# A new order of one attention unit on all five engines: the output projection a unit later and in another bank, the logits in the values' bank, no negation, GpSimd's row work in other places

## The reference, cut to what matters

```python
sa, ca, ga, sb, cb, gb = ...                   # from silu(c) @ wmod, per sequence; ga, gb kept away from 0
h = layernorm(x) * (1 + ca) + sa
Q, K, V = h @ Wq.T + bq, h @ Wk.T + bk, h @ Wv.T + bv     # 16 heads of 16; rotary positions on Q, K
weights = softmax(where(causal, Q @ K.T / 4, -1e9))
x = x + ga * ((weights @ V) @ Wo.T + bo)
h = layernorm(x) * (1 + cb) + sb
route = softmax(h @ switch_w + switch_b)       # 8 logits a token; the largest picks the expert
x = x + gb * (gelu(h @ w1[e] + b1[e]) @ w2[e] + b2[e]) * max(route)
```

## Time and profile before

| | |
|---|---|
| median of 3 runs | 783.38 us (782.95 to 783.81) |
| profiled execution, its own time | 782.81 us, span 781.0 us |
| mean granted clock of TensorE | 0.956 |
| busy, share of the span: TensorE | 677.4 us, 87% |
| VectorE | 601.2 us, 77% |
| ScalarE | 513.3 us, 66% |
| GpSimd | 475.3 us, 61% |

### The profile page before, as it was taken

How to read it: one execution, slowest core, us unless ns; L and a number is a source line. 1 busy time by engine, 2 the same in 40 slices (tenths; PEclk the granted TensorE clock), 3 DMA queues, 4 the chain that set the end, 5 groups by cost and what they waited for, 6 DMA issues and landing times. The chain is left out here.

```text
span 781.0 us, 21181 instructions
## 1 busy us (share of the span) xinstructions
PE 677.4 (87%) x7438; PEld 425.6 (55%) x7438; DVE 601.2 (77%) x1241; ACT 513.3 (66%) x1035; POOL 475.3 (61%) x609
## 2 busy tenths in 40 slices
PE   5766888899999999999999888855999999999993
PEld 4332444445454544545445444434787878788772
DVE  6577888989988989989889667248577777777774
ACT  2334888888888988889888878643444444444441
POOL 4422566788888888888978777841244453535331
PEclk9797999999999999999999999956999999999998
DMA  8103423334445543634536345339666642322100
GB/s 265 37 8 50 124 88 103 102 102 150 123 138 134 147 136 105 174 98 136 136 83 164 107 138 153 110 134 376 208 217 204 211 151 70 88 85 86 35 21 0
DMA packets 61363, 97.49 MB, mean 125 GB/s; under 512 B 8404, under 2 KB 42317, under 8 KB 60752
## 3 DMA queue, kind: packets, MB, share of 16 engines
q1 hardware_dynamic: 56272, 79.36, 34.5%
q0 software_dynamic: 4992, 16.79, 6.8%
HBM read 69.47 MB, written 34.51 MB: 133 GB/s over the span
## 5 line engine op out<-in xcount | busy, mean ns | idle before, releaser
L1150 DVE TENSOR_REDUCE row_max<-ps_max 128x2 f32<-128x768 f32 (+2 forms) x192 | 199.9, 1041 | 40.4 <-PE ps_max L672 40.3
L955 ACT ACTIVATE prob<-ps_sc 128x1024 f32<-128x1024 f32 (+1 forms) x192 | 169.7, 884 | 52.8 <-PE ps_sc L699 49.6
L1503 PE MATMUL ps_h<-tok_t,w_all 128*128 128x128 f16 x1872 | 156.3, 219 | 0.7 <-DVE tok_t L1678 0.5
L1503 PEld LDWEIGHTS ps_h<-tok_t,w_all 128*128 x1872 | 130.9, 98 | 41.9 <-issue 2.2
L1573 ACT ACTIVATE hid<-ps_h,b_t 128x128 f32<-128x128 f32 x312 | 89.3, 368 | 95.8 <-PE ps_h L1503 95.7
L441 POOL TENSOR_SCALAR_AFFINE_SELECT prob<-prob 128x512 f32<-128x512 f32 x128 | 87.0, 680 | 68.7 <-ACT prob L955 65.9
L1420 POOL DMA_INDIRECT slot_mem<-row_dram,token x39 | 55.8, 1430 | 119.3 <-DVE y L1713 99.4
L1516 PE MATMUL ps_y<-w_all,hid_parts 128*128 x312 | 118.0, 379 | 1.3 <-DVE hid_parts L1688 1.2
L665 PE MATMUL ps_max<-k_t,q_t 64*128 64x512 f16 (+3 forms) x512 | 69.0, 306 | 35.1 <-DVE row_max L1150 34.8
L712 PE MATMUL ps_pv<-prob,v_sb 128*32 128x512 f32 (+3 forms) x1024 | 90.3, 448 | 0.3
L1518 PE MATMUL ps_y<-w_all,hid_parts 128*128 x312 | 85.1, 273 | 0.0
(11 more groups left out here) (267 smaller groups left out, 1355.8 us busy)
## 6 DMA issues: line engine op xcount, KB each, us to landing
raw<-w SPq DMA_DIRECT2D x64, 256.0 KB, 3.0
w_dram<-halves SPq DMA_DIRECT2D x64, 256.0 KB, 3.3
w_all<-w_dram SPq DMA_DIRECT2D x20, 512.0 KB, 4.5
row_dram<-rows SPq DMA_DIRECT2D x32, 256.0 KB, 3.3
w_all<-w_dram SPq DMA_DIRECT2D x3, 2048.0 KB, 13.1
mod_rows<-mods_dram SPq DMA_DIRECT2D x16, 256.0 KB, 7.1
row_dram<-mods_dram SPq DMA_DIRECT2D x32, 128.0 KB, 4.8
xs<-x SPq DMA_DIRECT2D x24, 128.0 KB, 3.3
```

The lines of the kernel that those rows point to most:

```text
L955: nc.scalar.activation(p_kb[:, :, first * L:(first + n) * L], ps_sc[:, :, 0:n * L], ACT.Exp, scale=SCALE).then_inc(exp_done, 1)
L1150: nc.vector.tensor_reduce(dst, ps_max[:, :, 0:n * L].rearrange("p j (m l) -> p j m l", m=n), AX.X, ALU.max).then_inc(max_done, 1)
L1503: last = mm(o, w[:, :, k, f, :][:, bass.ds(e, 1), :].rearrange("p e m -> p (e m)"), tok_t[:, j % 2, piece, k, :], start=(n == 0 and f % HF ...
```

## The change

It reorders pieces of a unit and changes what they wait for:

- `project_out` and `residual` of a tile come a unit later, at s = 2 and s = 3, in columns of the query/key bank `ps_b` and not of `ps_nd`. The projection waits until the rotary work has read `ps_b`, and `q_transposes` until the residual has.
- The logits go to s = 4 and 5 of the unit before, in the values' bank `ps_a`.
- `maxima` writes into `q_aug` itself; the `negated` step is gone and the keys' constant column holds -1 instead of 1.
- The bias product of the query/key projection goes ahead to s = 0. On VectorE `statistics` goes to s = 0, `divide` to s = 2 and `residual` to s = 3. On ScalarE the second scaling of the second weight piece goes behind `keep_shift`.
- GpSimd: the unit begins with the former unit's last `low_piece`, then `low_h`, `row_power`, `row_hat`; `row_modulate` stands behind `rotate`; `gate_weights` and `add_const` stand behind `low_piece(2 * U)`, ahead of `clear_future(2)`.

The diff, cut to its core:

```diff
@@ GpSimd, setup
-            nc.gpsimd.memset(k_aug[:, :].rearrange("p (h w) -> p h w", w=HW)[:, :, 3 * DK:3 * DK + 1], 1.0).then_inc(consts_done, 1)
+            nc.gpsimd.memset(k_aug[:, :].rearrange("p (h w) -> p h w", w=HW)[:, :, 3 * DK:3 * DK + 1], -1.0).then_inc(consts_done, 1)
@@ GpSimd, units
             for U in range(NU):
-                T = U + LEAD
-                if U >= QT - 1:
-                    add_const(U - QT + 1)
+                T, Y = U + LEAD, U - QT - 2
+                if U:
+                    low_piece(2 * U - 1)
+                if U and T < NT:
+                    low_h(T)
+                if Y >= 0:
+                    row_power(Y)
+                    row_hat(Y)
                 clear_future(U, 0)
-                if U % QT >= QT - KC:
-                    gate_weights(U // QT, U % QT - QT + KC)
                 if T < NT:
                     rotate(T)
+                if Y >= 0:
+                    row_modulate(Y)
                 if T + 1 < NT:
                     rstd_of(T + 1)
                 clear_future(U, 1)
                 low_piece(2 * U)
+                if U % QT >= QT - KC:
+                    gate_weights(U // QT, U % QT - QT + KC)
+                if U >= QT - 1:
+                    add_const(U - QT + 1)
                 clear_future(U, 2)
                 clear_future(U, 3)
...
-                low_piece(2 * U + 1)
-                if U >= QT + 1:
-                    row_power(U - QT - 1)
-                    row_hat(U - QT - 1)
-                if T + 1 < NT:
-                    low_h(T + 1)
-                if U >= QT + 1:
-                    row_modulate(U - QT - 1)
@@ TensorE, units
                     scores(U, s)
-                    if s == 0 and U:
-                        weigh(U - 1, 2)
-                        weigh(U - 1, 3)
-                    if s == 1 and Z > 0 and Z % QT == 0:
-                        pe.wait_ge(x1_done, X)
-                        logit_products(Z // QT - 1, ps_nd)
...
+                    if s == 0:
+                        if U:
+                            weigh(U - 1, 2)
+                            weigh(U - 1, 3)
+                        if T < NT:
+                            project_bias(ps_b[:, :], T)
+                    if s == 1:
+                        if T < NT:
+                            for part in range(2):
+                                project_qk(T, part, ps_b[:, :])
+                        if Z >= 0:
+                            ge(pe, att_kept, X)
+                            h_transposes(Z, ps_nd)
                     if s == 2:
...
                         if U:
                             tokens_first(U - 1)
+                        if X > 0:
+                            if T < NT:
+                                pe.wait_ge(rope_done, 3 * T + 3)
+                            project_out(X - 1, ps_b[:, :])
...
                         weigh(U, 1)
+                        if Z >= 0 and Z % QT == QT - 1:
+                            if T < NT:
+                                pe.wait_ge(v_kept, T + 1)
+                            logit_products(Z // QT, ps_a)
                     if s == 5:
-                        if X >= 0:
-                            project_out(X, ps_nd)
+                        if Z >= 0 and Z % QT == QT - 1:
+                            logit_transposes(Z // QT, ps_a)
+                        if U == NU - 1:
+                            pe.wait_ge(x1_done, X)
+                            project_out(X, ps_b[:, :])
                         if T < NT:
+                            ge(pe, x1_done, X)
                             q_transposes(T, ps_b[:, :])
@@ ScalarE, units
                     if s == 4 and X >= 0:
                         keep_att(X, ps_nd)
+                    if s == 4 and Z >= 0 and Z % QT == QT - 1:
+                        keep_logit_t(Z // QT, ps_a)
+                if Z >= 0 and Z % QT == QT - 1:
+                    keep_logits(Z // QT, ps_a)
                 high_piece(2 * U + 1)
                 if V < NU:
                     keep_shift(V)
+                scaled_piece(2 * U + 1)
@@ VectorE
-                dst = row_max[:, V % 2, qt, :].rearrange("p (m j) -> p j m", j=2)[:, :, first:first + n]
+                par, g = place(V)
+                column = q_aug[:, par, qt, :].rearrange("p (h w) -> p h w", w=HW)[:, HG * g:HG * (g + 1), 3 * DK]
+                dst = column.rearrange("p (m j) -> p j m", j=2)[:, :, first:first + n]
...
-                    if s == 0 and X > 0:
-                        residual(X - 1, ps_nd)
-                    if s == 1 and T + 1 < NT:
+                    if s == 0 and T + 1 < NT:
                         statistics(T + 1)
                     if s == 1 and T < NT:
                         rope(T, ps_b[:, :])
-                    if s == 3 and U:
+                    if s == 2 and U:
                         divide(U - 1)
+                    if s == 3 and X > 0:
+                        residual(X - 1, ps_b)
...
-                if V < NU:
-                    negated(V)
```

More of the change, by code:

```diff
@@ L534, in _ @@
                 low_piece(2 * U)
+                if U % QT >= QT - KC:
+                    gate_weights(U // QT, U % QT - QT + KC)
+                if U >= QT - 1:
+                    add_const(U - QT + 1)
                 clear_future(U, 2)
                 clear_future(U, 3)
-                if U == NU - 1:
-                    for X in range(NT - QT + 1, NT):
-                        add_const(X)
-                low_piece(2 * U + 1)
-                if U >= QT + 1:
-                    row_power(U - QT - 1)
-                    row_hat(U - QT - 1)
-                if T + 1 < NT:
-                    low_h(T + 1)
-                if U >= QT + 1:
-                    row_modulate(U - QT - 1)
+            for X in range(NT - QT + 1, NT):
+                add_const(X)
+            low_piece(2 * NU - 1)
+            row_power(NT - QT - 2)
+            row_hat(NT - QT - 2)
+            row_modulate(NT - QT - 2)
             first = NT - QT
@@ L609, in x_transposes, with project_bias, project_qk @@
                 last.then_inc(xt_ps, 1)
-            def project_qk(T, part, ps, kept_before):
+            def project_bias(ps, kept_before):
+                ge(pe, qt_kept, kept_before)
+                mm(ps, ones3[:, :], bias3[:, 0:2 * D], start=True, stop=False)
+            def project_qk(T, part, ps):
                 if part == 0:
                     pe.wait_ge(h_high, T + 1)
-                    ge(pe, qt_kept, kept_before)
-                    mm(ps, ones3[:, :], bias3[:, 0:2 * D], start=True, stop=False)
                     for k in range(KC):
@@ L775, in _ @@
                 ps_q, ps_v = lead_banks(T)
+                project_bias(ps_q, T - 1)
                 for part in range(2):
-                    project_qk(T, part, ps_q, T - 1)
+                    project_qk(T, part, ps_q)
                 project_v(T, ps_v, T - 1)
@@ L815, in _ @@
                     scores(U, s)
-                    if s == 0 and U:
-                        weigh(U - 1, 2)
-                        weigh(U - 1, 3)
-                    if s == 1 and Z > 0 and Z % QT == 0:
-                        pe.wait_ge(x1_done, X)
-                        logit_products(Z // QT - 1, ps_nd)
-                    if s == 1 and T < NT:
-                        for part in range(2):
-                            project_qk(T, part, ps_b[:, :], T)
-                    if s == 1 and Z > 0 and Z % QT == 0:
-                        logit_transposes(Z // QT - 1, ps_nd)
-                    if Z >= 0 and s == h_shot(Z):
-                        ge(pe, logits_kept, Z // QT)
-                        pe.wait_ge(x1_done, X)
-                        h_transposes(Z, ps_nd)
+                    if s == 0:
[11 more added lines that the diff above has]
+                            h_transposes(Z, ps_nd)
                     if s == 2:
@@ L997, in _ @@
                         keep_u(U - 1)
-                    if s == 1 and Z > 0 and Z % QT == 0:
-                        keep_logit_t(Z // QT - 1, ps_nd)
-                        keep_logits(Z // QT - 1, ps_nd)
-                    if Z >= 0 and s == h_shot(Z):
+                    if s == 1 and Z >= 0:
                         keep_h(Z, ps_nd)
@@ L1271, in _ @@
             first = NT - QT
-            residual(first - 1, ps_nd)
+            residual(first - 1, ps_b)
             row_statistics(first - 1)
```

26 lines of the change are left out of this document (11 added, 15 removed).

## The result

The changed kernel takes **787.3 us** (median; 785.26 to 790.45 over 7 runs) where the kernel before takes 783.38 (781.1 to 784.94 over 7 runs beside it): 1.0054 times as long, 95% interval 1.0036 to 1.0071. Slower, as forecast, but by 4 us and not by 25. Its profiled execution has a span of 785.1 us against 781.0, at a granted clock of 0.957 against 0.956.

A forecast was written before the change was run, and what follows sets the result against it. No engine has room; the path runs through TensorE into the fourth maximum, down VectorE to the negation, then into the next unit. Units 6 to 25 +11.7 and +18.7, logits -3.4, first units +1.5, end -3.7: +24.8, forecast 808, range 772 to 820.

The forecast's parts named there:

- it waited for the end of the whole row, not for one instruction: VectorE's normalisation waits out GpSimd's row: +1.1 us a unit, +1.8 with gate_weights; likeliest case, chance 0.46.
- the wait lasts one instruction: Rival: normalisation goes in behind clear_future(2) or add_const, about +0.45 and +0.55 a unit; total 787, chance 0.20.
- Alternation of the low parts: VectorE's low parts alternate with GpSimd's work: low part 0.25, add_const 0.69, low part 0.25, then clear_future(2).
- Projection, +0.3: On TensorE the output projection ahead of the fourth maximum's products delays that maximum by 0.3 us; bounds -0.3 to +1.1.
- Moves put at nothing: ScalarE's second scaling, statistics, division, residual, weight pieces' loads and stores, and later x1: no cost on the path.
- Negation, -0.23: Removing VectorE's negation takes 0.20 plus a 0.03 gap off the path, -0.23 us a unit.
- Logits, -0.85: Logits leaving s = 1 save 0.85 us in each of units 11, 15, 19, 23 (bounds 0.58 and 1.09): -3.4.
- The gap that I named as a sign against it: An idle gap over 0.5 us before the rotary work in units 11, 15, 19, 23 would show the logits term wrong.
- Unit 27, -2.7: Unit 27, idling 2.30 us behind its logits before the third maximum, then at half the clock, saves 2.7 us.
- First six units, +1.5: Units 0 to 4 gain 0.5 us each, units 2 to 5 lose 1.0 each to GpSimd's new row: together +1.5.
- Clock: Rival: TensorE's clock falls after idling nearly 2 us, up to 1.6 in each of ten units; up to 824, chance 0.09.
- No collision, the other side, 775: Rival: the normalisation finds a gap in GpSimd's row at t = 9.5 to 12; change gains 8.2 us, chance 0.20.

The follow-up runs named there:

- e8: Kernel after with three 128x768 bf16 memsets on GpSimd between add_const and clear_future(2): 853.64 us, 1.0895 of the kernel before.
- e9: Kernel after with GpSimd waiting for its own memset behind each of the first two large setup memsets: 785.29 us, one run.
- e10: Kernel after with three 128x768 bf16 GpSimd copies between add_const and clear_future(2): 806.13 us, 1.0266 of the kernel before.
- e5: Kernel after with one of the two products of each output projection row block left out: 787.32 us, 1.0055 of the kernel before.
- e6: Kernel after with add_const and gate_weights behind clear_future(3), and clear_future(2) waiting for the normalisation: 764.19 us, 0.975 of the kernel before.
- e12: e6 with one of the two products of each output projection left out: 760.17 us, 0.9684 of the kernel before.
- e3: Kernel before with the negation alone taken out: 782.71 us, 0.999 of the kernel before.
- e2: Kernel after with add_const and gate_weights moved behind clear_future(3), to the end of GpSimd's row: 773.12 us, 0.9864 of the kernel before.
- e7: Kernel before with add_const and gate_weights moved behind low_piece and the negation taken out: 797.86 us, 1.0177 of the kernel before.
- e11: Kernel before with clear_future(2) waiting for the normalisation, nothing else changed: 782.18 us, 0.9968 of the kernel before.
- e4: Kernel after with three 128x256 bf16 memsets on GpSimd between clear_future(2) and clear_future(3): 786.14 us, 1.0048 of the kernel before.
- e1: Kernel before with GpSimd's add_const and gate_weights moved behind low_piece(2U): 828.34 us, 1.056 of the kernel before.

## Why the prediction was wrong, step by step

- **The step that failed**: "it waited for the end of the whole row, not for one instruction", carried over from the setup's memsets to GpSimd's work in a unit: the normalisation was to end behind clear_future(3), **+1.1** a unit, and **+1.8** with gate_weights. It ends behind the one instruction in flight: at t = 11.45 instead of 12.1 in unit 17, 0.72 long, and 0.81 in units with gate_weights, where it gets in behind add_const. From the fifth maximum to the sixth the collision cost 0.58 in unit 17, and 0.53 to 0.70 in units 7 to 25. GpSimd's row up to there was drawn nearly as it came: clear_future(1) at t = 7.90 for 7.8, the end of low_piece at 9.66 for 9.52. (From 9.62, where the first low part was put, the drawn row would have ended at 12.05 and not at 11.95.) e8, e9 and e10 show why the setup's row misled: only rows of memsets held VectorE beyond the instruction in flight, and not even these each time.
- The second case, *the wait lasts one instruction*, had the mechanism and the time, 787, with +0.45 and +0.55 for the 0.58 measured in unit 17. That the total fits it so well is in part luck: the low clock in units 5 and 6 added some 1.8 that none of its terms holds, and the setup took 1.1 off. I gave it 0.20, since I set one row of another operation above the row of the nearer kind. The rule of the Trainium skill, "SBUF — State Buffer", section "Who interferes with whom", that the one that starts first keeps the shared pair for its whole instruction, agrees with this trace: 0.72 here, 0.91 among copies. For rows of memsets the measurement differs (1.97 over the rest of three), and decides. The same section of the Trainium skill says that a VectorE instruction with two SBUF inputs does not contend with one of GpSimd that only writes; the multiplication at 5.05 in e9 took 0.41 beside a memset, which agrees.
- **Alternation of the low parts**: right. The second waits for add_const, as drawn.
- **Projection, +0.3**: the fourth maximum came at t = 6.55 instead of 6.41, so +0.14, and even that was not on the path, since in e5, with a fourth maximum earlier still, the unit stayed at 14.08. GpSimd's row up to the end of low_piece sets the stretch behind it.
- **Moves put at nothing**: one of them was not nothing. ScalarE's second scaling now stands behind the shift copies (row 319.84), and GpSimd's row begins with the low_piece that needs it: in unit 17 it waits 2.29 us for the scaling and starts within 0.1 of its end (row 320.56). From its start at 306.47 GpSimd works on to clear_future(3) without a wait above 0.2 us. So shift copies, scaling, GpSimd's row, low parts and sixth maximum wait for each other in a ring, once around in a unit, and a cheaper projection does not shorten that ring; in e6 and e12 GpSimd's row starts within 0.1 of the scaling's end, too. No run moves the scaling alone, so what its place costs is not shown.
- **Negation, -0.23**: alone worth nothing (e3), because a second path, TensorE's projection and the query transposes into VectorE's copy, ended with it. That "the path runs through TensorE into the fourth maximum, stays on VectorE down to the negation" was half of the truth. The projection's move away from the unit's end should make the removal count in the new order, but that is argued and not shown: no run has the new order with the negation in it.
- **Logits, -0.85**: units 11, 15, 19, 23 went from 14.66 to 14.22; as the collision adds some 0.6 there, the logits gave about 1.05 (an estimate from these two), within the bounds. The gap that I named as a sign against it, 0.59 before unit 15's rotary work, did stand there; unit 17 has 0.51 too, so it comes from the new order and not from logits.
- **Unit 27, -2.7**: 14.13 to 11.58, -2.55, right, and the low clock behind it is gone. Units 28 and 29: 11.16 for 11.29.
- **First six units, +1.5**: +0.84 (84.54 us from the start of unit 0 to that of unit 6, before 83.70), and 0.9 of it is the low clock of unit 5, below; without that, nothing. That unit 6 starts 0.27 earlier comes from the setup: unit 0 starts at 65.53 instead of 66.64, a time that lies between 64.7 and 68.5 in these kernels.
- **Clock**: it did fall once where it had not before. From 147 to 153 the granted clock is 0.72 in the mean of its two levels, 1.2 and 2.4 GHz; the key transposes at 148.06 take 0.90 instead of 0.61, behind waits of TensorE of 1.23 and 0.44, and units 5 and 6 take 14.88 and 15.05, each about 0.9 above their kind. Unit 17 has waits of 0.94 and 0.44 there and keeps the full clock, so the cause stays open.
- **No collision, the other side, 775**: not what happened, but what e2 reached by moving two calls.

The sum again with what was measured, units 6 to 25: ten units without gate_weights at about +0.5, four more with it at +0.6, unit 6 +1.5, unit 7 +0.1, the four that lost logits at -0.45: 5.0 + 2.4 + 1.5 + 0.1 - 1.8 = +7.2, against 7.04 in the trace.

## What to carry to other kernels

When GpSimd work moves, look first at which VectorE instructions with two SBUF inputs or plain SBUF-to-SBUF work it will run beside: each such meeting on the path cost the rest of one GpSimd instruction here, or of several where these were memsets, and a wait that parked GpSimd for 1.01 us took 0.44 off the unit. Before a stall row is carried over, check that it is of the same kind of instruction; and before an instruction on the path is priced at its full length, look for the path that ends at the same moment, since taking out the negation, worth nothing alone (e3), was worth 30 us in another order (e7), and a wait worth 0.06 a unit in the old order (e11) was worth 0.44 in the new one (e6). A move of an off-path instruction can close a new path too, as the scaling did.

## What the runs showed of the hardware that was not expected

- Memsets of GpSimd in a row mostly hold VectorE's tensor_scalar to the end of the row (1.97 us in e8, 25 of 26 times; 3.55 in the setup), three copies do not (0.91 in e10), and a semaphore wait between two memsets ended the hold (0.52 in e9). Three shorter memsets in e4 let it in behind the second, all three times that it was issued among them (0.45). What decides stays open.
- The 128x16 negation, 0.20 us of work, took up to 1.149 beside a low_piece (e1): what a meeting costs goes by the other engine's instruction, not by one's own.
